# Feed-forward layers of a two-layer block: the residual is added between the scale steps and the rounding, and ScalarE makes the normalised input of the next tile

## The reference

```python
def fp4_quant_dequant(x):                     # blocks of 16 along the last dim
    scale = jnp.maximum(jnp.max(jnp.abs(xb), -1, keepdims=True) / 6.0, 1e-12)
    xn = xb / scale
    q = _GRID[jnp.searchsorted(_MID, jnp.abs(xn))] * jnp.sign(xn) * scale
...
gate = fp4_linear(x, w_gate)                  # 256 -> 704, x and w both rounded
y = fp4_linear(x, w_up)                       # 256 -> 704
h = jax.nn.silu(gate) * y
return fp4_linear(h, w_down)                  # 704 -> 256
...
x = x + 0.5 * _L0_ffn_ref(_layernorm(x, axis=-1), w_gate, w_up, w_down)
```

## Time and profile before

| | before |
|---|---|
| median of 3 runs | 5151.13 us (5150.79 to 5154.98) |
| the profiled execution's own time | 5150.29 us |
| its span in the trace | 5148.7 us |
| PE busy | 3708.2 us (72%) |
| DVE busy | 3685.3 us (72%) |
| ACT busy | 2557.9 us (50%) |
| POOL busy | 2348.4 us (46%) |
| first ffn, first input tile to last residual | 92.7 to 411.0 us |
| second ffn, the same | 1858.2 to 2175.9 us |

### The profile page before, as it was taken

The page is one execution under the profiler, slowest core; times in us unless marked ns, Lnnn a source line. Parts: engine busy times, 40 slices in busy tenths (PEclk is TensorE's granted clock), DMA queues, the critical chain, the costliest instruction groups (busy, mean ns, idle before and its releaser), DMA issues. The chain is left out here.

```text
span 5148.7 us, 85718 instructions
## 1 busy us (share of the span) xinstructions
PE 3708.2 (72%) x28907; PEld 2589.2 (50%) x28907; DVE 3685.3 (72%) x4478; ACT 2557.9 (50%) x4164; POOL 2348.4 (46%) x1532
## 2 busy tenths in 40 slices
PE   2996645555555569849636898998888888885594
PEld 1663224444444446548613565565555555664483
DVE  6882589999999978820156887888878888875101
ACT  1222466666666622123113676777666666674121
POOL 0220278888888822120214655556656566600202
PEclk9998777777777789959858999999999999996697
DMA  2000001100101100026422222222222222202264
GB/s 84 0 0 5 6 23 31 31 29 29 31 29 31 29 22 0 20 84 193 132 88 57 54 53 47 47 49 69 52 63 52 51 52 55 52 4 90 79 192 132
DMA packets 237294, 276.27 MB, mean 54 GB/s; under 512 B 63771, under 2 KB 185556, under 8 KB 235536
## 3 DMA queue, kind: packets, MB, share of 16 engines
q1 hardware_dynamic: 224032, 244.85, 17.4%
q0 software_dynamic: 8704, 24.35, 1.4%
q10 hardware_dynamic: 4224, 2.76, 0.2%
HBM read 152.60 MB, written 36.04 MB: 37 GB/s over the span
## 5 line engine op out<-in xcount | busy, mean ns | idle before, releaser
L2197 DVE TENSOR_TENSOR att_b_prob_low<-att_b_prob,att_b_prob_high 128x1024 f16<-128x1024 f32 (+2 forms) x640 | 765.5, 1196 | 188.7 <-ACT att_b_prob_high L2158 156.3
L2164 ACT ACTIVATE att_b_prob<-att_b_score,att_soft 128x1024 f32<-128x1024 f32 (+2 forms) x640 | 631.7, 987 | 195.5 <-PE att_b_score L2069 121.5
L2224 DVE TENSOR_REDUCE att_b_neg_max<-att_b_peek 128x1 f32<-128x1024 f32 (+1 forms) x748 | 667.3, 906 | 71.5 <-PE att_b_peek L2046 55.4
L1037 PE MATMUL mix_scan_hT<-ident,mix_scan_h 128*128 128x128 f32 x1024 | 248.7, 390 | 535.1 <-DVE mix_scan_h L985 501.2
L2158 ACT CAST att_b_prob_high<-att_b_prob 128x1024 f16<-128x1024 f32 (+2 forms) x640 | 588.1, 919 | 32.8 <-PE att_b_o L2097 15.5
L2093 PE MATMUL att_b_o<-att_b_vh,att_b_prob_high 128*128 128x65 f16 x4352 | 462.8, 195 | 95.1 <-DVE att_b_heads L2215 54.7
L2093 PEld LDWEIGHTS att_b_o<-att_b_vh,att_b_prob_high 128*128 128x128 f16 x4352 | 399.2, 98 | 217.7 <-DVE att_b_prob_low L2197 129.3
L1037 PEld LDWEIGHTS mix_scan_hT<-ident,mix_scan_h 128*128 128x128 f32 x1024 | 172.1, 197 | 649.4 <-DVE mix_scan_h L985 443.8
L2095 PE MATMUL att_b_o<-att_b_vl,att_b_prob_high 128*128 128x64 f16 x4352 | 460.6, 193 | 0.0
L2097 PE MATMUL att_b_o<-att_b_vh,att_b_prob_low 128*128 128x65 f16 x4352 | 460.4, 194 | 0.0
L2067 PE MATMUL att_b_score<-att_b_q_both,att_b_k_twice 128*128 128x512 f16 (+3 forms) x1280 | 448.2, 350 | 8.9 <-issue 7.3
(11 more groups left out here) (339 smaller groups left out, 9526.5 us busy)
## 6 DMA issues: line engine op xcount, KB each, us to landing
moe_w<-in_L_ffn_W_dram SPq DMA_DIRECT2D x64, 1024.0 KB, 8.0
mix_scan_b_row<-mix_b_rows SPq DMA_DIRECT2D x128, 256.0 KB, 3.2
att_b_crossed<-att_b_raw SPq DMA_DIRECT2D x512, 64.0 KB, 2.0
att_b_q_both<-att_b_halves SPq DMA_DIRECT2D x240, 64.0 KB, 2.0
att_b_k_twice<-att_b_halves SPq DMA_DIRECT2D x240, 64.0 KB, 2.0
moe_slots_in<-moe_route_zero SPq DMA_DIRECT2D x2, 4096.0 KB, 14.3
moe_exp_x<-moe_slots_in SPq DMA_DIRECT2D x32, 256.0 KB, 4.3
moe_slots_out<-moe_exp_y POOLq DMA_DIRECT2D x32, 256.0 KB, 6.6
```

What stands on the lines that cost most here:

```text
L1037: last = pe.transpose(hT_ps[:, j * D + m * P:j * D + (m + 1) * P], hs[:, b * W + m * GRP + t * P:b * W + m * GRP + (t + 1) * P], ident[:, :])
L2164: act.activation(prob[:, at:at + width], score[m % 2][:, 0:width], ACT.Exp, scale=soft[:, 0:1])\
L2197: dve.tensor_tensor(prob_low[:, at:at + width], prob[:, at:at + width], prob_high[:, at:at + width], ALU.subtract).then_inc(low_ready, 1)
L2224: last = dve.tensor_reduce(neg_max[:, first + col:first + col + 1], peek_bank(kind, s)[:, base:base + nb * P], AX.X, ALU.max, negate=True)
```

## The change

`fp4_round` is cut in two. `fp4_scales` holds its first four steps (L177 to L181), and `fp4_round` the last five. In `ffn`, VectorE's slot becomes: silu(gate)*up, the waits, `fp4_scales`, `add_back` of tile t-2, `fp4_round`. The multiply of `src` into `y` counts up a semaphore of its own, `y_made`, instead of the chain's; `ffn_weights` gets such a semaphore too (`made`).

The normalised input is made by ScalarE, at the head of its slot t, for tile t+2, after waiting until VectorE has read `src` in its slot t-1 (`y_made`). It computes X*rstd + shift, with shift = -mean*rstd, two small VectorE instructions once per call.

```diff
+            c.link(dve.tensor_tensor(shift[:, :], norm["mean"][:, :], norm["rstd"][:, :], ALU.mult))
+            dve.tensor_scalar(shift[:, :], shift[:, :], -1.0, None, ALU.mult).then_inc(shift_ready, 1)
 
             def slot(t, b, has_x, has_h):
-                if has_x:
-                    dve.tensor_scalar(src[:, FFN:], X[:, rows(t + 2)], norm["mean"][:, bass.ds(t + 2, 1)],
-                                      norm["rstd"][:, bass.ds(t + 2, 1)], ALU.subtract, ALU.mult)\
-                        .then_inc(xn_ready, 1)
                 if has_h:
...
-                if not (isinstance(t, int) and t < 2):
-                    add_back(t - 2)
                 wait_unless_first(dve, rounded, t + 2)
                 wait_unless_first(dve, xq_ready, t + 1 if has_x else NT)
                 wait_unless_first(dve, hq_ready, t - 1)
...
+                here = src[:, first * QB:(first + nb) * QB]
+                fp4_scales(dve, c, here, amax, scale[:, b * NB + first:(b + 1) * NB], inv, nb)
+                if not (isinstance(t, int) and t < 2):
+                    add_back(t - 2)
+                last = fp4_round(dve, c, here, y[:, b * BOTH + first * QB:(b + 1) * BOTH], step, inv, nb, y_made, t + 3)
...
         def _(act):
             norm_scalar(nc, act, norm)
+            act.wait_ge(shift_ready, 1)
+
+            def normed(t):
+                act.activation(src[:, FFN:], X[:, rows(t)], ACT.Identity, scale=norm["rstd"][:, bass.ds(t, 1)],
+                               bias=shift[:, bass.ds(t, 1)]).then_inc(xn_ready, 1)
 
             def slot(t, b, has_x, has_h):
                 if has_x:
+                    wait_unless_first(act, y_made, t + 2)
+                    normed(t + 2)
                     act.wait_ge(x_turned, t + 3)
```

More of the change, by code:

```diff
@@ L166, with fp4_scales, fp4_round @@
 FP4_STEPS = 9
-def fp4_round(dve, c, src, y, step, amax, scale, inv, nb, parts=P):
+def fp4_scales(dve, c, src, amax, scale, inv, nb, parts=P):
+    amax, sc, iv = amax[0:parts, 0:nb], scale[0:parts, 0:nb], inv[0:parts, 0:nb]
+    c.link(dve.tensor_reduce(amax, src.rearrange("p (n b) -> p n b", b=QB), AX.X, ALU.max, apply_absolute_value=True))
+    c.link(dve.tensor_scalar(sc, amax, 1.0 / 6.0, 1e-12, ALU.mult, ALU.max))
+    c.link(dve.reciprocal(iv, sc))
+    c.link(dve.tensor_scalar(iv, iv, 1.0 - 2.0 ** -23, None, ALU.mult))
+def fp4_round(dve, c, src, y, step, inv, nb, made, count, parts=P):
     blocks = lambda ap: ap.rearrange("p (n b) -> p n b", b=QB)
@@ L175, in fp4_round @@
     y, step = y[0:parts, 0:nb * QB], step[0:parts, 0:nb * QB]
[L176 to L182, removed]
+    dve.tensor_tensor(blocks(y), blocks(src), wide(inv), ALU.mult).then_inc(made, 1)
+    dve.wait_ge(made, count)
     c.link(dve.tensor_scalar(step.bitcast(I32), y.bitcast(I32), 0x7F800000, None, ALU.bitwise_and))
@@ L194, in fp4_scaled, with fp4 @@
                              scale[0:parts, 0:nb].unsqueeze(2).to_broadcast([parts, nb, QB]), ALU.mult)
-def fp4(dve, c, src, dst, y, step, amax, scale, inv, nb, parts=P):
-    c.link(fp4_round(dve, c, src, y, step, amax, scale, inv, nb, parts))
+def fp4(dve, c, src, dst, y, step, amax, scale, inv, nb, made, count, parts=P):
+    fp4_scales(dve, c, src, amax, scale, inv, nb, parts)
+    c.link(fp4_round(dve, c, src, y, step, inv, nb, made, count, parts))
     return fp4_scaled(dve, y, scale, dst, nb, parts)
@@ L217, in ffn_weights @@
         turned = [ctx.enter_context(nc.psum_tensor(f"w_turned{i}", [P, 1024], F32)) for i in range(2)]
-        loaded, quant, turn, copied, chain, stored, cleared = map(
-            sem, ("w_loaded", "w_quantised", "w_turned_s", "w_copied", "w_chain", "w_stored", "w_cleared"))
+        loaded, made, quant, turn, copied, chain, stored, cleared = map(
+            sem, ("w_loaded", "w_made", "w_quantised", "w_turned_s", "w_copied", "w_chain", "w_stored", "w_cleared"))
         block = ctx.enter_context(nc.Block())
@@ L256, in _ @@
                 dst = wq[0:size, (n % 2) * FULL:(n % 2) * FULL + width]
-                fp4(dve, c, src[0:size, first:first + width], dst, y, step, amax, scale, inv, width // QB, size)\
+                fp4(dve, c, src[0:size, first:first + width], dst, y, step, amax, scale, inv, width // QB, made, n + 1, size)\
                     .then_inc(quant, 1)
@@ L328, in ffn @@
                 "silu_ready", "h_taken", "h_turned", "hT_ready", "out_ready", "added", "chain"))
+        shift = sb("shift", [P, NT])
+        shift_ready, y_made = sem("shift_ready"), sem("y_made")
         block = ctx.enter_context(nc.Block())
@@ L363, in slot @@
                     dve.wait_ge(h_taken, 2 * t + 2)
-                c.start((t + 2) * (FP4_STEPS - 1))
+                c.start((t + 2) * (FP4_STEPS - 2) + 1)
                 first, nb = (0 if has_h else NH), (NB if has_x and has_h else NH if has_h else NB - NH)
[L366 to L369, removed]
+                here = src[:, first * QB:(first + nb) * QB]
[3 more added lines that the diff above has]
+                last = fp4_round(dve, c, here, y[:, b * BOTH + first * QB:(b + 1) * BOTH], step, inv, nb, y_made, t + 3)
+                assert c.n == FP4_STEPS - 2
                 last.then_inc(rounded, 1)
```

## The result

The changed kernel takes 5601.88 us (median of 5 runs, 5595.18 to 5604.74), against 5150.79 for the kernel before in the same runs: a ratio of 1.0879, 95% interval 1.0864 to 1.0894. It is 8.8% slower; the forecast was 5499, with a range that ended at 5600.

A forecast was written before the change was run, and what follows sets the result against it. TensorE was taken as the bound before, at 9.35 us a slot; the change makes a serial loop of 14.19. 5150.3 + 293 for the longer calls + 55 for the clock = 5498, forecast 5499 us, range 5436 to 5600.

The forecast's parts named there:

- The loop: In ffn's steady slots, the late Identity makes the engines wait in series: 14.19 us a slot in place of 9.35.
- Three signs: In ffn's slots: VectorE's block maximum waits about 5 us for the Identity; busy shares fall to about 0.6 VectorE, 0.65 TensorE.
- transposes to gate: On TensorE, from the input transposes to the gate matmuls: 0.97 us of the loop.
- gate to first silu: From TensorE's gate matmuls to ScalarE's first silu: 2.76 us of the loop.
- first silu to scale steps: ScalarE's silu through the last hidden copy 1.61 us, Identity 0.50, then 0.03 to VectorE's start.
- The ends: Each ffn call outside its steady slots: first slots 7.6 us longer, tail 1.5 us shorter.
- the tail: End of each ffn call, after the last slot's transposes: 1.5 us shorter than before.
- The clock: TensorE's idle 3.8 us a slot lowers its clock in a bit over half the slots, 1.70 us each: +55 us.
- a rival (2.6 a slot, 5595 us): Serial loop with TensorE's clock down nearly always, 2.6 us in each slot: 5595 us, chance 0.18.
- No table is loaded for the Identity: Rival on ScalarE: Identity between silu loads a table in each slot, 1.28 us: 5573 us, chance 0.03.
- The Identity was late: Rival on ScalarE: the Identity is not late, TensorE's 9.35 us slot stays: no change, 5151 us, chance 0.04.
- VectorE was not the bound: Rival: VectorE bounds ffn, so the residual's 0.68 us wait comes out of each slot: 5112 us, chance 0.03.

The follow-up runs named there:

- r_only: Only the residual moved behind the scale steps, VectorE still making the normalised input, against the kernel before: 5146.68 us, ratio 0.9989.
- early: The changed kernel with ScalarE's Identity one slot earlier, making tile t+3 at the head of slot t: 5144.41 us, ratio 0.9983 to the kernel before.
- awake_both: The changed kernel plus unread matmuls per TensorE slot, four before the input transposes and three before the output matmuls: 5470.54 us, ratio 1.0633 to the kernel before.
- fill_mid: The changed kernel plus three unread matmuls per slot, only between the up and the output matmuls: 5614.81 us, ratio 1.0903 to the kernel before.
- i_only: Only the Identity moved to ScalarE, the residual back ahead of the rounding's waits, against the kernel before: 5563.11 us, ratio 1.0793.
- awake_two: The changed kernel plus two unread matmuls per slot, only before the input transposes: 5495.13 us, ratio 1.0678 to the kernel before.

## Why the prediction was right or wrong

**The bound and the loop: right.** TensorE was the bound, and taking work off VectorE alone moved nothing (r_only, early). The loop was forecast as 14.19 us; with the clock held up it has 14.38. Three signs were put too low or too high: VectorE's wait was to be about 5 us, and is 5.9 with the clock held up (142.2 us in 24 slots of awake_both) and 8.5 with it down; VectorE's share was to be 0.6 and TensorE's 0.65, and they are 0.48 and 0.71 (214.53 and 319.49 of 450), in the longer slot with the slower matmuls. The terms against the slot of the changed kernel at 307.73 (us):

| term | forecast | measured |
|---|---|---|
| transposes to gate | 0.97 | 1.15 |
| gate to first silu | 2.76 | 5.18 |
| first silu to scale steps | 1.61 + 0.50 + 0.03 | 2.22 |
| scale steps and residual | 2.54 | 2.67 |
| multiply to end of rounding | 4.93 | 4.93 |
| end of rounding to transposes | 0.85 | 0.91 |

All but the first two are within 0.13; these two have the transposes and the gate at the low level, 0.69 and 5.06 us in place of 0.44 and 2.63. VectorE starts 0.13 after the Identity's end and not 0.03, and the residual in the middle of the chain costs 0.16 of waiting beside its 0.34.

**The ends: nearly.** The transposes of slot 0 came 8.7 us later, not 7.6, since the gate of the slot before (4.15 us) was slow too; the tail was 1.1 longer instead of 1.5 shorter, because its last gate was slow. At the full clock I had +293; awake_both measured +311.9, of which 0.19 x 58 = 11 are the loop and the other 8 the ends.

**The clock: this step failed.** The step was "I take 1.70 in a bit over half the slots: 0.95 x 58 = +55". Both factors were too small. The gates are slow in all steady slots, and whole: 5.06 - 2.63 = 2.43, and the transposes and what hangs on them make 17.06 - 14.38 = 2.68. Over 58 slots that is 155 at most; between the two kernels it measured 149. 149 - 55 = 94 us is nearly all of the 103 by which 5602 lies above 5499; the 19 of loop and ends add to it, and the other stages, 7 shorter in the profiled execution, take from it. I had this as a rival (2.6 a slot, 5595 us) with a chance of 0.18, and had the range end just above it, short of the 5602 that came.

The error in the reasoning was to take a stretch of 3.8 us (3.7 in the trace), against the 4.33 where a fall was seen, for a coin toss, and the part of a gate that was slow in slot 0 for its price. The runs show a sharper thing: with this thin stretch (the changed kernel, fill_mid) every steady gate is at the low level; with two fillers in it some are, with four none. One reading, not tested, is that the fall sustains itself: a slow gate makes the loop longer and leaves the idle stretch as long as it was, so nothing in the slot works against the next fall. The Trainium skill's account (TensorE: Matmul & The Clock Gate, section "HAM oscillation — how this bites in real kernels"), a fall in every iteration, is what this kernel does; the forecast named it and gave it too little.

Why the steady slots all look alike (5.06 each), where i_only goes round four different ones, the runs don't settle. The length of the thin stretch alone doesn't explain it: i_only's is longer (5.4 to 5.8 us against 3.7), and its gates are at times less slow. No run varied the length of the loop alone.

**The rivals.** No table is loaded for the Identity: in the first call of the changed kernel (95 to 400 us) ScalarE has one load, ahead of a silu, and hidden copy, Identity and next copy follow with no load between. The Identity was late, as the 8.5 us of VectorE's wait say. VectorE was not the bound, and so r_only and early gained no more than 0.2%.

## What to carry to other kernels

Before moving an instruction to an engine with time to spare, write down what stands ahead of it in that engine's order and whose slot that work belongs to: the engine was busy a fifth of the time, and VectorE still waited 8.5 us in each slot for the instruction (5.9 without the slow clock), because it stood behind work of the other engines' current slot. The cure was its place, not its engine. When a loop turns serial, count the clock as part of the price from the start: in the changed kernel, fill_mid and i_only, where TensorE has a stretch of 3.7 to 5.8 us with nothing but transposes in every slot, the gate was slow in every steady slot, in whole or in part. Only when the stretch was partly filled (awake_two) was it slow in a share of them.

## What the runs showed of the hardware

Three fillers in a 2.1 us stretch changed no gate; two in the stretch before the gate brought back 17 of 28. Seven added matmuls a slot whose result nothing reads made the changed kernel 2.3% faster (1.0633 against 1.0879). A gate wholly at the 1.2 GHz level (granted clock 0.50) takes 5.06 us against 2.63 at the 2.4 GHz level, a ratio of 1.92.
